# Expert weights of a decoder layer: split once at the end of attention, or a sixteenth per attention tile with a copy in DRAM

## The reference

```python
x = x + attn(layernorm(x), Wq, bq, Wv, bv, anomaly_matrix)   # softmax over 2048 keys
x = x + xattn(layernorm(x), ctx, mask, Wq, Wkv, Wo)          # 4 heads, softmax over 1601 keys
# ffn(layernorm(x)):
idx = argmax(softmax(x @ Wg + bg))                           # one expert of 4 per token
h = gelu(einsum('bld,edf->belf', x, W1) + b1)                # W1: 4 x 256 x 1024
y = einsum('belf,efd->beld', h, W2) + b2                     # W2: 4 x 1024 x 256
x = x + y[idx]
```

## Time and profile before

| | us |
|---|---|
| three runs | 841.83, 843.75, 843.74 |
| median | 843.74 |
| span of the profiled execution | 848.8 |
| TensorE busy in it | 755.1 (89%) |
| VectorE busy | 653.2 (77%) |
| ScalarE busy | 457.9 (54%) |
| GpSimd busy | 138.9 (16%) |

### The profile page before, as it was taken

How to read it: one execution, slowest core, us unless ns; L and a number is a source line. 1 busy time by engine, 2 the same in 40 slices (tenths; PEclk the granted TensorE clock), 3 DMA queues, 4 the chain that set the end, 5 groups by cost and what they waited for, 6 DMA issues and landing times. The chain is left out here.

```text
span 848.8 us, 19493 instructions
## 1 busy us (share of the span) xinstructions
PE 755.1 (89%) x6136; PEld 681.1 (80%) x6137; DVE 653.2 (77%) x1619; ACT 457.9 (54%) x922; POOL 138.9 (16%) x246
## 2 busy tenths in 40 slices
PE   3988799999999999999999999999986416999996
PEld 2778689989889899898898998988975314999995
DVE  5984647788888888888888888888878465777773
ACT  2544626566566665666666656666665432334332
POOL 3100110120211201202112012021120410222221
PEclk9999989999999999999999999999978856999999
DMA  6242110010101000000010000000123260111110
GB/s 211 70 138 70 47 29 7 24 29 15 29 12 28 28 6 28 24 16 28 12 28 28 6 28 24 17 28 12 54 113 99 101 235 26 36 39 39 37 33 15
DMA packets 25525, 39.32 MB, mean 46 GB/s; under 512 B 3086, under 2 KB 18704, under 8 KB 25360
## 3 DMA queue, kind: packets, MB, share of 16 engines
q1 hardware_dynamic: 23232, 33.02, 12.5%
q0 software_dynamic: 2256, 5.83, 2.0%
HBM read 28.82 MB, written 10.41 MB: 46 GB/s over the span
## 5 line engine op out<-in xcount | busy, mean ns | idle before, releaser
L1076 ACT ACTIVATE ps_cross<-flip 128x512 f16<-128x512 f32 (+1 forms) x256 | 125.0, 514 | 116.5 <-PE flip L795 91.0
L1318 DVE TENSOR_TENSOR ps_cross<-flip,ps_cross 128x512 f16<-128x512 f32 (+1 forms) x256 | 145.0, 583 | 24.8 <-ACT ps_cross L1076 20.4
L795 PE MATMUL flip<-ident,exp_cross 128*128 128x128 f32 (+1 forms) x832 | 131.8, 282 | 9.9 <-DVE ps_cross L1318 6.5
L1277 ACT ACTIVATE exp_cross<-exp_cross,xneg 128x1024 f32<-128x1024 f32 (+1 forms) x128 | 122.7, 960 | 19.2 <-DVE xneg L1492 19.1
L784 PE MATMUL scores<-keys_cross,qt 128*128 128x402 f32 x512 | 127.6, 372 | 5.3 <-DVE xneg L1492 3.5
L795 PEld LDWEIGHTS flip<-ident,exp_cross 128*128 128x128 f32 (+1 forms) x832 | 95.8, 143 | 18.1 <-DVE ps_cross L1318 8.3
L672 PE MATMUL scores<-keys_self,u_tile 128*128 128x512 f32 x384 | 102.2, 403 | 6.4 <-issue 4.9
L806 PE MATMUL cross_out<-vals_cross,ps_cross 128*128 128x128 f16 (+1 forms) x832 | 102.5, 224 | 5.5 <-issue 4.9
L771 PE MATMUL flip<-vals_self,ps_self 128*128 128x256 f32 x768 | 103.8, 289 | 0.0
L806 PEld LDWEIGHTS cross_out<-vals_cross,ps_cross 128*128 128x128 f16 (+1 forms) x832 | 76.4, 101 | 28.3 <-issue 20.4
L771 PEld LDWEIGHTS flip<-vals_self,ps_self 128*128 128x128 f32 x768 | 96.7, 194 | 0.0
(11 more groups left out here) (207 smaller groups left out, 1189.2 us busy)
## 6 DMA issues: line engine op xcount, KB each, us to landing
w_stage<-W SPq DMA_DIRECT2D x8, 1024.0 KB, 5.4
u_dram<-u_out SPq DMA_DIRECT2D x4, 1024.0 KB, 5.9
u_tile<-u_dram SPq DMA_DIRECT2D x16, 256.0 KB, 2.7
mask_tile<-mask SPq DMA_DIRECT2D x16, 200.1 KB, 2.4
rows<-rows_dram SPq DMA_DIRECT2D x19, 130.0 KB, 2.1
x_all<-x SPq DMA_DIRECT2D x4, 512.0 KB, 5.8
x_tile<-x SPq DMA_DIRECT2D x16, 128.0 KB, 2.0
b_row<-b SPq DMA_DIRECT2D x1, 2048.0 KB, 8.9
```

Of the source, the lines that this page charges most:

```text
L795: tr = pe.transpose(flip[0:rows, bank(use), n * P:(n + 1) * P], exp_cross[:, h % 2, m * P:m * P + rows], ident[:, :])
L1076: return act.activation(out, in_, ACT.Copy, **kw)
L1277: act.activation(exp_cross[:, h % 2, cols], exp_cross[:, h % 2, cols], ACT.Exp, bias=xneg[:, h % 2, 1:2], scale=-1.0, accum_out=xden[:, ha ...
L1318: return dve.tensor_tensor(out, full, hi, ALU.subtract)
```

## The change

Each of bodies 0 to 15 gets a sixteenth of the weights (a "piece": 256 KB of W1 and 256 KB of W2). SP loads it into `w_piece`, ScalarE writes its high part to `w_high`, GpSimd subtracts in place so that `w_piece` holds the low part, and SP writes both to `w1_dram` and `w2_dram`. The piece of body j+1 is loaded after the writes of body j have landed and `x1_ready` of body j has come.

After body 15, SP loads the finished parts straight into `w1s` and `w2s`, in 16 DMAs of 1 MB: W1 of experts 0 and 1 when the last self-attention scores are done, of experts 2 and 3 and the biases after the last `x1_ready`, W2 of experts 0 to 2 after the last cross-attention scores, and of expert 3 after the last use of `ps_cross`. `weights_hi`, `weights_lo` and `w_stage` are gone.

For room, `ps_self` has three buffers instead of four (the fourth group of a tile takes the first's), and `o_tile`, `x3t` and `ot` lie in `qs` and `xt`. The weights of one expert lie side by side, so that one offset serves both products; it is a fourth row of `table`, which costs VectorE two more small operations.

```diff
+        def load_piece(t):
+            sp.dma_start(w_piece[:, 0, :]..., w1_pieces[bass.ds(t, 1), :, :]...).then_inc(piece_loaded, 16)
+            sp.dma_start(w_piece[:, 1, :]..., w2_pieces[bass.ds(t, 1), :, :, :]...).then_inc(piece_loaded, 16)
+        def keep_piece(t):
+            for part, held in ((0, w_high), (1, w_piece)):
+                sp.dma_start(w1_dram[part, bass.ds(t, 1), :, :]..., held[:, 0, :]...).then_inc(piece_kept, 16)
+                sp.dma_start(w2_dram[part, bass.ds(t, 1), :, :]..., held[:, 1, :]...).then_inc(piece_kept, 16)
...
+            if k < T:
+                sp.wait_ge(piece_hi, j + 1)
+                sp.wait_ge(piece_lo, j + 1)
+                keep_piece(j)
+            if k < T - 1:
                 sp.wait_ge(x1_ready, j + 1)
                 loads_x(j + 1)
+                sp.wait_ge(piece_kept, 64 * (j + 1))
+                load_piece(j + 1)
...
+            if a:                                          # GpSimd, after norm_col
+                pool.wait_ge(piece_hi, j + 1)
+                pool.tensor_tensor(w_piece[:, :, :], w_piece[:, :, :].bitcast(F32), w_high[:, :, :].bitcast(F32),
+                                   ALU.subtract).then_inc(piece_lo, 1)
...
+        def piece_high(j):                                 # ScalarE
+            act.wait_ge(piece_loaded, 32 * (j + 1))
+            copy(w_high[:, :, :], w_piece[:, :, :].bitcast(F32)).then_inc(piece_hi, 1)
...
-            if k == T:
-                weights_hi(0)
+            if a:
+                piece_high(j)
...
-            if k == T:
-                weights_lo(0)
...
+            if g == 3:
+                act.wait_ge(self_p_used, 4 * j + 1)
+            elif k >= 1:
+                act.wait_ge(self_p_used, 4 * j if g == 0 else 4 * j + g - 3)
```

More of the change, by code:

```diff
@@ L47 @@
 NOBODY = 65536.0
+WE = 2 * C * DF
 NG = -(-MC // 4)
@@ L195, in emit @@
     exp_self = sb("exp_self", [P, N], F32, loop)
-    ps_self = sb("ps_self", [P, 4, 2, 512], F32R, loop)
+    ps_self = sb("ps_self", [P, 3, 2, 512], F32R, loop)
+    w_piece = sb("w_piece", [P, 2, 512], F32R, loop)
+    w_high = sb("w_high", [P, 2, 512], F32R, loop)
     mask_tile = sb("mask_tile", [P, M], U8, loop)
@@ L206, in emit @@
     qt = sb("qt", [P, H, P], F32R, loop)
-    o_tile = sb("o_tile", [P, H, HD], F32, loop)
-    ot = sb("ot", [P, 2, C, P], F32R, loop)
+    o_tile = qs[:, 0:2, :, :].bitcast(F32).rearrange("p a two d -> p (a two) d")
+    ot = xt
     xn3 = sb("xn3", [P, D], F32, loop)
-    x3t = sb("x3t", [P, C, P], F32, loop)
+    x3t = qs[:, 2:4, :, :].bitcast(F32).rearrange("p c two d -> p c (two d)")
     bs1 = sb("bs1", [P, 6], F32, loop)
@@ new lines, in _, with load_w1, load_w2 @@
+        w1_parts = w1_dram.rearrange("two (e c q) (r s) f -> two e c (q r) (s f)", e=E, c=C, s=2)
+        w2_parts = w2_dram.rearrange("two (e q) p f -> two e q p f", e=E)
+        def load_w1(e):
+            whole = w1s[:, e * WE:(e + 1) * WE].bitcast(F32).rearrange("p (two c f) -> p two c f", two=2, c=C)
+            for part in range(2):
+                sp.dma_start(whole[:, part, :, :], w1_parts[part, e, :, :, :].rearrange("c p f -> p c f")).then_inc(w1_loaded, 16)
+        def load_w2(e):
+            whole = w2s[:, e * WE:(e + 1) * WE].bitcast(F32).rearrange("p (two q f) -> p two q f", two=2, q=4)
+            for part in range(2):
+                sp.dma_start(whole[:, part, :, :], w2_parts[part, e, :, :, :].rearrange("q p f -> p q f")).then_inc(w2_loaded, 16)
@@ new lines, in _ @@
+        sp.wait_ge(piece_kept, 64 * T)
+        sp.wait_ge(scores_ready, 4 * T)
+        load_w1(0)
+        load_w1(1)
+        sp.wait_ge(x1_ready, T)
+        load_w1(2)
+        load_w1(3)
+        sp.dma_start(b1_row[:, :], bass.AP(io["b1"].tensor, 0, [[0, P], [1, E * DF]])).then_inc(b_loaded, 16)
+        sp.dma_start(b2_row[:, :], bass.AP(io["b2"].tensor, 0, [[0, P], [1, E * D]])).then_inc(b_loaded, 16)
+        sp.wait_ge(cross_scores_ready, 8 * T)
+        for e in range(E - 1):
+            load_w2(e)
@@ L1282, in _ @@
         copy(barrier[:, 0:1], ident[:, 0:1]).then_inc(attention_done, 1)
-        for n in (E + 2, E + 3):
-            weights_hi(n)
         act.wait_ge(attention_done, 3)
@@ L1474, in self_lo @@
             dve.wait_ge(self_p_hi, 4 * j + g + 1)
-            low(ps_self[:, g, 1, :], flip[:, bank(("s", g)), :], ps_self[:, g, 0, :].bitcast(F32)).then_inc(self_p_lo, 1)
+            low(ps_self[:, g % 3, 1, :], flip[:, bank(("s", g)), :], ps_self[:, g % 3, 0, :].bitcast(F32)).then_inc(self_p_lo, 1)
         def part_max(j, k, n):
@@ L1779, in blocks @@
                 x_lo_f(0)
-                for n in range(E + 2, 2 * E):
-                    weights_lo(n)
                 statistics(b + 1, 1)
```

120 lines of the change are left out of this document (36 added, 84 removed).

## The result

| | before | after |
|---|---|---|
| median | 843.75 us (841.83 to 844.14) | 876.64 us (874.33 to 880.53) |
| profiled span | 848.8 us | 878.4 us |
| granted clock, mean in the profiled execution | 0.954 | 0.942 |

The ratio is 1.0402, 95% interval 1.0371 to 1.0433. I had forecast 831.3, 0.985. What came instead is the mechanism of rival 1 (I gave it 7% and 862 us): GpSimd's new subtraction locks VectorE out in the loop.

What follows compares the result with a forecast made beforehand. TensorE, busy 89% of the span, was taken to bound the kernel, with waits behind weight copies late on. Gains of 10.5+0.9+1.0 = 12.4 us, loop cost 0, gave 831.3 from 843.74; range 824.5 to 839.5, about 80%.

Steps and rivals of the forecast that it cites:

- rival 1: Loop: GpSimd's subtraction blocks VectorE in every body, low part 2 to 2.5 us late in 14 bodies; 862 us; 7%.
- The subtraction's cost in the loop: Loop: GpSimd's subtraction takes 1 to 3 us, within 13.0 us of idle time per body, so it costs 0.
- From 0.9 us a body: Loop: the loss per body from which GpSimd blocking VectorE would decide the outcome.
- ScalarE's copy and the traffic in the loop: Loop: a copy of 1.0 to 1.1 us in ScalarE's idle time and the pieces' DMAs cost 0; loop bounds 0 and +3.
- perhaps 1 us: First body: ScalarE's copy waits for its piece and the first exponential stands behind it, costing about this much.
- Body 16: Body 16: removing four W1 pairs gains 10.5 us, 9.8 of shifts and 0.7 for TensorE's clock.
- rival 4: From 603 us: full DMA engines delay routing or padding DMAs and L615; some 4 us lost, 835; 6%.
- Body 17: Body 17: without two W2 pairs the low part no longer delays GpSimd's power L615; 0.9 us gained.
- slack of 7.86 us: GpSimd's time before power L615, so only a larger delay of routing or padding DMAs would count.
- First expert blocks: First expert block: without two W2 low parts holding VectorE, the second bias moves from 713.2 to 712.2; 1.0 us gained.
- Sum: Whole kernel: gains of 10.5+0.9+1.0 = 12.4 us, median from 843.74 to 831.3.
- Rival 3: Body 17's unexplained pause goes and the clock stays up: 4.7 us more gained, 826.6; 13%.

Runs made afterwards that it cites:

- second profile of before: The kernel before, unchanged, profiled once more: span 841.9 us, without the first profile's TensorE pauses in body 17.

## Why the prediction was wrong, step by step

**The subtraction's cost in the loop: wrong, 48 us in the profile and 44 by medians.** This is the step that failed: "cost 0", for a subtraction that would only use GpSimd's idle time. I priced GpSimd's side well: 1 to 3 us taken, 2.35 measured (the estimate from the Trainium skill, GPSIMD Engine Reference, section 3.1 Elementwise, was 2.3); it idles 14.4 us before the power and no one waits for its result. What does not follow from that is "cost 0": the runs show 2.0 us of TensorE waiting for `ps_cross` and 1.7 us at 1.2 GHz behind it, in 13 bodies. With it the weight of rival 1 was wrong. I had the collision: the right instructions, the right place, even the row of an addition held up to the end of the mask bias. I then let one reciprocal of 0.18 us speak for the multiplication behind it. The reciprocal is of a kind that passes; the multiplication, and the addition of my own rows 8, are not. Four elements are no shelter: the lock lasts as long as GpSimd's instruction, not as long as VectorE's.

**Rival 1's price: 862, measured 876.6.** It was the waits alone, 31 us for 14 bodies. Measured were 13 bodies (in body 2 the subtraction is over before `xcoef`), 2.0 us of wait each where I had 2 to 2.5, and 1.7 us more for the stretch at 1.2 GHz that I had not put behind it. "From 0.9 us a body" was nearly right: in the run with half the subtraction 1.0 us a body ate the gain, 844.5.

**ScalarE's copy and the traffic in the loop: right.** The copy takes 1.05 us, `qs` on ScalarE still waits 1.1 us for its product, and the body without the subtraction has 34.02 us. Up to the last `x1` that kernel is 1.1 us longer than the second profile of before (611.13 for 610.03), and the one with the subtraction late but in body 0 is 1.7 longer (611.77), inside the bounds of 0 and 3. Whether the first body pays "perhaps 1 us" stays open: its `x1` stands at 115.43 after, at 115.05 and 114.66 in the two profiles before, and anywhere from 114.29 to 116.95 in the others with the pieces.

**Body 16: right in sum, 10.9 for 10.5, but by errors that cancel.** From the last `x1` to the last `cross_max` of body 16, the second profile of before has 661.67-610.03 = 51.6 us and the one after 699.71-658.98 = 40.7. This is the main part of the gain. Pair by pair it did not come as forecast. Counted from the last `x1`, the starts of `cross_max` behind the first, second, third and fourth pair moved by 0.3, 3.8, 7.1 and 10.9 us (23.43 to 23.16, 28.15 to 24.34, 41.04 to 33.91, 51.64 to 40.73), where I had 1.4, 4.9, 7.0 and 10.5. The low part of `qs` did come 1.4 us earlier (16.28 for 17.65). The `cross_max` behind it then had a new wait, GpSimd and VectorE after:
```profile
679.37 0.40 POOL L629 COPY record<-x_old 128x256 f32<-128x256 f32 x1 [6.01 <-issue]
...
682.14 1.00 DVE L1508 CUSTOM_DVE_ANT_0 exp_cross<-scores,mask_bias 128x804 f32<-128x804 f32 x1 [1.49 <-POOL mask_bias L640]
```
While W1 loads, the routing DMA of body 16 lands after 6.0 us instead of 1.7, the mask bias comes late, and most of the first pair's gain is lost to it (the profile names no releaser for the 6.0 us; in the program this copy waits for the semaphore of that DMA). The third pair gave 3.3 us where I had counted 2.1 of its 3.0, which made up for it. The mechanism of rival 4 was thus at work in body 16 already.

**Body 17: wrong in sign, 1 us.** The low part no longer stretches L615's power (0.59 us), as said. But from the last `cross_max` to the first flip of `xn_f` it takes 36.7 us after (699.71 to 736.43) and 36.1 before (661.67 to 697.76): 0.6 lost where I had 0.9 gained. Rival 4's mechanism was there: the routing DMA landed late behind the weights, and VectorE waited for the power:
```profile
721.58 0.41 DVE L1613 TENSOR_SCALAR xn<-record,mv,rs 128x256 f32<-128x256 f32 x1 [3.78 <-POOL rs L662]
```
My slack of 7.86 us belonged to the pauses of that one execution; in the second profile it is 1.29. And I had counted slack from the landing of the weights, not what they do to small transfers on the way.

**First expert blocks: 2.2 for 1.0.** From that flip to the end, 144.1 before and 142.0 after. The first block is 0.7 us shorter and the second 0.9 (5.23 to 4.55 and 3.79 to 2.94 us between TensorE's steps). The third step is 0.75 us shorter (3.65 to 2.90), which makes up the rest. Its product and the window of each, before (second profile) and after:
```profile
709.48 3.81 PE L672 MATMUL scores<-w1s,xt_f 128*128 x12
...
708.00:710.00 2.00, 2.00 (x9) 1.57 (x8) 1.63 (x5) 1.36 (x3) 0.69 (x2) 0.50 0.00 0
```
```profile
746.63 3.06 PE L719 MATMUL scores<-w1s,xt_f 128*128 x12 [0.56 <-issue]
...
747.00:749.00 2.00, 2.00 (x10) 1.65 (x9) 1.28 (x3) 0.00 (x0) 0.00 (x0) 1.00 0.00 0
```
So part of the gain is the granted clock, 0.50 there before and 1.00 after, which I had put at nothing in this stage.

**Sum.** 10.9-0.6+2.2 = 12.5 against my 12.4. That they agree is luck: body 17 and the first blocks miss in opposite directions, and so do the pairs in body 16. By medians the two kernels without the lock gain 11.2 and 11.5, because the loop takes the 1.1 and 1.7 us above. **Rival 3** drew on a pause that was no part of the kernel.

## What to carry to other kernels

An instruction added to an idle GpSimd was free here only where VectorE issued nothing beside it that reads two tiles in SBUF, or one in a TENSOR_SCALAR (of four elements; a single one passed): look at what VectorE's order holds in exactly those microseconds, four-element operations included, and put the instruction beside operations that read PSUM. When one row speaks for a lock and one against, compare their kinds before weighing them. Moved to VectorE the same subtraction holds up GpSimd, so follow GpSimd's results too. And a stop of TensorE is to be priced with the clock behind it.

## What was not expected of the hardware

- A stop of 2.0 us cost 3.7 us and one of 1.0 us cost 1.0: only after the longer one was the granted clock 0.50 for some 3.5 us, in 49 of 52 cases; after the other three it stayed at 1.00 and the stop cost 2.1 to 2.2.
- In all 13 bodies VectorE's locked operation of four elements ended within 0.04 us of GpSimd's instruction, 2.32 to 2.33 us long; half the subtraction made it 1.24 to 1.26.
- The routing DMA of one tile, for which GpSimd waits 1.7 to 1.9 us, took 6.0 in bodies 16 and 17, while the weight loads moved 320 to 455 GB/s in the windows of 2 us (703 to 711 and 672 to 678).
